# Keys and values of two cross attentions: projected for all batches at once in split fp32r and kept in DRAM, instead of batch by batch in fp32

## What is computed

```
q = (x @ Wq)                       # 256 -> 16 heads of 64
k = (context @ Wk); v = (context @ Wv)   # 192 -> 1024, 77 rows per batch
attn = softmax(q k^T / 8)
out = (attn v) @ Wo + bo
x = layernorm(x + out)
```

## Time and profile before

| what | value |
|---|---|
| median of 3 runs | 1628.12 us |
| the three runs | 1628.12, 1632.04, 1611.5 us |
| profiled execution, first to last instruction | 1625.5 us |
| busy: TensorE matmul (PE) | 1396.0 us, 86% |
| busy: weight load (PEld) | 1133.9 us, 70% |
| busy: VectorE (DVE) | 986.7 us, 61% |
| busy: ScalarE (ACT) | 637.4 us, 39% |
| busy: GpSimd (POOL) | 421.8 us, 26% |
| DMA moved | 82.25 MB, mean 51 GB/s |

### The profile page before, as it was taken

How to read it: one execution, slowest core, us unless ns; L and a number is a source line. 1 busy time by engine, 2 the same in 40 slices (tenths; PEclk the granted TensorE clock), 3 DMA queues, 4 the chain that set the end, 5 groups by cost and what they waited for, 6 DMA issues and landing times.

```text
span 1625.5 us, 28296 instructions
## 1 busy us (share of the span) xinstructions
PE 1396.0 (86%) x12184; PEld 1133.9 (70%) x12184; DVE 986.7 (61%) x1739; ACT 637.4 (39%) x743; POOL 421.8 (26%) x434
## 2 busy tenths in 40 slices
PE   5899998998969999996799699879979957878885
PEld 5688887887848889995488468748756845556553
DVE  5766756756636446776555836765583646556563
ACT  3554344434532335652344245234424511422413
POOL 2230120300311744664024412702421240000000
PEclk9999999999979999998799899979999977977868
DMA  9100000000040225872000100100000020111000
GB/s 378 61 1 1 1 1 1 1 1 1 1 181 27 77 80 193 280 228 72 1 1 32 34 1 1 61 6 1 21 20 1 1 117 2 40 29 39 2 14 14
DMA packets 28493, 82.25 MB, mean 51 GB/s; under 512 B 3152, under 2 KB 13008, under 8 KB 27344
## 3 DMA queue, kind: packets, MB, share of 16 engines
q1 hardware_dynamic: 25296, 72.05, 12.4%
q0 software_dynamic: 3072, 8.39, 1.6%
HBM read 53.95 MB, written 26.48 MB: 49 GB/s over the span
## 4 chain that ended last, share of the span: by engine, by line
PE 33%; DVE 15%; ACT 3%; POOL 2%; issue 1%; DMA 0%; POOLq 0%; DVEq 0%; ACTq 0%; another core or an unknown queue 0%
DVE sm L1520 7%; PE ps L644 5%; PE ps L1008 4%; PE ps L1014 4%; PE ps L114 3%; PE ps L116 3%; PE ps L115 3%; PE ps L989 2%; PE ps L759 2%; DVE m L1509 2%; PE ps L775 2%; PE ps L656 2%; PE ps L1128 2%; DVE m L1896 1%; ACT m L1188 1%
## 5 line engine op out<-in xcount | busy, mean ns | idle before, releaser
L1188 ACT ACTIVATE m<-ps 128x1024 f32<-128x1024 f32 (+4 forms) x248 | 183.9, 758 | 342.1 <-PE ps L116 156.3
L1520 DVE TENSOR_REDUCE sm<-ps 128x8 f32<-128x2048 f32 (+1 forms) x128 | 193.5, 1531 | 44.3 <-PE ps L989 42.6
L2124 POOL TENSOR_SCALAR sm<-sm 128x2 f32<-128x2 f32 x40 | 8.7, 218 | 764.5 <-DVE sm L1538 764.5
L1509 DVE TENSOR_TENSOR r<-ps,r 128x512 fp32r<-128x512 f32 (+1 forms) x159 | 116.2, 739 | 138.9 <-ACT r L1188 136.6
L1188 ACT ACTIVATE r<-ps 128x512 fp32r<-128x512 f32 (+1 forms) x159 | 101.3, 640 | 237.4 <-PE ps L644 117.6
L1406 ACT ACTIVATE m<-ps 128x2048 f32<-128x2048 f32 x64 | 119.6, 1877 | 150.7 <-PE ps L1008 150.7
L644 PE MATMUL ps<-cst,m 128*77 128x128 f32 (+2 forms) x1024 | 143.1, 281 | 26.6 <-ACT m L1188 5.6
L644 PEld LDWEIGHTS ps<-cst,m 128*77 128x77 f32 (+2 forms) x1024 | 116.0, 148 | 60.1 <-issue 20.2
L114 PE MATMUL ps<-r,w0h 128*128 128x256 f32 (+1 forms) x416 | 122.2, 294 | 17.9 <-DVE r L1509 13.6
L989 PE MATMUL ps<-m 32*128 32x256 f32 x1024 | 104.0, 545 | 37.2 <-DVE sm L1520 22.2
L115 PE MATMUL ps<-r,w0h 128*128 128x256 f32 (+1 forms) x416 | 118.9, 286 | 0.0
(11 more groups left out here) (241 smaller groups left out, 3603.5 us busy)
## 6 DMA issues: line engine op xcount, KB each, us to landing
raw<-wu_dram SPq DMA_DIRECT2D x20, 768.0 KB
keep_dram<-m SPq DMA_DIRECT2D x8, 768.0 KB, 3.2
m<-keep_dram SPq DMA_DIRECT2D x8, 768.0 KB, 4.9
xs_dram<-small SPq DMA_DIRECT2D x2, 2944.0 KB, 32.8
ys_dram<-m SPq DMA_DIRECT2D x23, 256.0 KB, 3.1
room<-wu_dram SPq DMA_DIRECT2D x7, 768.0 KB, 5.5
rt<-xs_dram SPq DMA_DIRECT2D x16, 256.0 KB, 3.7
w1raw<-w_dram SPq DMA_DIRECT2D x1, 3840.0 KB, 15.2
```

Of the source, the lines that this page charges most:

```text
L1188: return act.activation(o, i, ACT.Copy)
L1509: return dve.tensor_tensor(o, a, b_, op)
L1520: return dve.tensor_reduce(o, i, AX.X, op, **kw)
```

## The change

The context of all eight batches (616 columns, padded to 640) is loaded once as `ctxA` and `ctxB`, split into high and low parts, and the weights Wk and Wv are loaded raw and split, for layer 0 in the places of `wq` and `wo` (which are loaded and split after it), for layer 1 over the first 4096 columns of the same tile. `keys_values(L, u)` computes unit u of nine: units 0 to 3 are keys (four pieces of 308 columns each), units 4 to 8 are values (two pieces of 512 columns each); every piece is `mm5`, five fp32r matmuls. That is 16 pieces of keys and 10 of values per layer. Each piece is copied from PSUM to one of three slots of `stage`, and each unit is stored to DRAM (`kd`, `vd`); each batch loads its K (two DMAs) and V (one) back.

In layer 0 the nine units stand where the values and keys of batches 0 and 1 stood; batches 2 to 7 have empty steps there. In layer 1 all nine stand behind the last step of the first stage, with ACT copying and one bank in four in turn; POOL and ACT split their weights in `xattn` of batch 7. The second stage has empty steps where values and keys stood, V has a tile of its own and K lies in `w1f`, set to zero once.

The file defines the three tables twice. The first `FIRST` and `SECOND` have new numbers; behind them stands the line `CT = mybir.ActivationFunctionType` and then the constants and the tables again, with the numbers of the kernel before. Python keeps the second definition, so the program's steps run in the order of the old tables; `CT` is set to 640 further down.

```diff
+FIRST = {
+    "POOL": [0, 3, 5, 10, 11, 11, 12, 12, 12, 12, 12, 12, 13, 16, 17, 20, 21],
...
+CT = mybir.ActivationFunctionType
...
-CP = 78
-CW = 98
+CT = 640
+KW = CK * B // 2
+NSLOT = 3
+SLOT = 2 * B * CK
...
+def mm5(pe, o, a, b, ab, bb):
+    pe.matmul(o, a[0], b[0], start=True, stop=False)
+    pe.matmul(o, a[0], b[1], start=False, stop=False)
+    pe.matmul(o, a[1], b[0], start=False, stop=False)
+    for i, (l, r) in enumerate((l, r) for l in ab for r in bb):
+        m = pe.matmul(o, l, r, start=False, stop=i == 1)
+    return m
...
+            v.V = st.v1[0:CK, :] if L else m[0:CK, 0:1024]
+            v.Kf = w1f[:, 1232 * st.i:1232 * st.i + 1232] if L else m[:, 1024:2256]
+            v.K = v.Kf.rearrange("p (h c n) -> p c h n", h=2, c=8)
...
+            def store_kv(L, u):
+                slot, done, _ = slot_of(L, u)
+                sp.wait_ge(*kv_ev[L].at(L, u, 3 if u < 4 else 1))
+                if u < 4:
+                    sp.dma_start(kd[L].rearrange("b p n -> p b n")[:, :, 154 * u:154 * u + 154], slot.rearrange("p (b n) -> p b n", b=B)).then_inc(done, 16)
+                else:
+                    sp.dma_start(vd[L, P * (u - 4):P * (u - 3), :], slot[:, 0:1024]).then_inc(done, 16)
+
+            def stored(L):
+                for i in range(NSLOT):
+                    sp.wait_ge(d_slot[i], 16 * 3 * (L + 1))
+
+            def load_kv(L, b):
+                st = streams[b % 2]
+                v = x_views(st, L)
+                for h in range(2):
+                    r = slice(64 * h, 64 * h + 64)
+                    sp.dma_start(v.Kf[r, 616 * h:616 * h + 616], kd[L, b, r, :]).then_inc(d_kv[L][st.i], 16)
+                sp.dma_start(v.V, vd[L, CK * b:CK * b + CK, :]).then_inc(d_kv[L][st.i], 16)
...
+            load_kw("k0", P0["wq"][0], 0, 2048)
+            load_kw("v0", P0["wo"][0], 2048, 2048)
             load0("wout")
-            sp.dma_start(ctxT[:, 0:3 * B * CP], ctx_in).then_inc(d_ctx, 16)
-            sp.dma_start(w0f[:, 280:], w0f_in[:, 280:]).then_inc(d_kv, 16)
             sp.dma_start(xres[:, 4 * D:], x_in[:, 4 * D:]).then_inc(d_x[1], 16)
+            for u in range(4):
+                store_kv(0, u)
             load0("wq")
+            for u in range(4, 9):
+                store_kv(0, u)
             load0("wo")
+            stored(0)
+            for b in range(2):
+                sp.wait_ge(*streams[b].x_pool[0].at(b, "kz"))
+                load_kv(0, b)
...
+            for b in range(2, B):
+                sp.wait_ge(*streams[b % 2].x_pe[0].at(b - 2, "o3"))
+                load_kv(0, b)
+            for st in streams:
+                sp.wait_ge(*st.l0_pe.at(st.batches[-1], "proj"))
+            load_kw("kv1", 0, 4096, 4096)
...
             fetch(0)
             fetch(1)
+            for u in range(9):
+                store_kv(1, u)
...
+            def keys_values(L, u):
+                for s in range(4 if u < 4 else 2):
+                    q = KVQ[L, u, s]
+                    o, turns = kv_bank(L, q), 4 if L else 2
+                    if q >= turns:
+                        pe.wait_ge(*kv_ev[L].at(*KVK[q - turns, L]))
+                    if u < 4:
+                        c, r = slice(128 * (2 * u + s // 2), 128 * (2 * u + s // 2) + 128), slice(KW * (s % 2), KW * (s % 2) + KW)
+                        wa, wb = kv_weights(L, 0)
+                        m = mm5(pe, o[:, 0:KW], cols(wa, A, c), cols(ctxA, A, r), cols(wb, A, c), (ctxB[:, r],))
+                    else:
+                        t, r = slice(128 * (u - 4), 128 * (u - 3)), slice(512 * s, 512 * s + 512)
+                        wa, wb = kv_weights(L, 1)
+                        m = mm5(pe, o, cols(ctxA, A, t), cols(wa, A, r), (ctxB[:, t],), cols(wb, A, r))
+                    m.then_inc(kv_pe.up(L, u, s), 1)
...
-                values(st, b, 0, bank(st, 1), 0)
-                yield
-                pe.wait_ge(*kv_done.at(b, "v0"))
-                values(st, b, 0, bank(st, 1), 1)
-                yield
-                pe.wait_ge(*kv_done.at(b, "v1"))
-                keys(st, b, 0, bank(st, 1), 0)
-                yield
-                pe.wait_ge(*st.l0_dve.at(b, "sp"))
-                keys(st, b, 0, bank(st, 2), 1)
-                yield
+                if b == 0:
+                    for i in range(2):
+                        pe.wait_ge(*streams[i].l0_act.at(i, "z"))
+                    pe.wait_ge(*ctx_s["lo"].at("b"))
+                    pe.wait_ge(*kw_s["lo"].at("k", 0))
+                elif b == 1:
+                    pe.wait_ge(*kw_s["lo"].at("v", 0))
+                for us in ([0], [1], [2], [3]) if b == 0 else ([4, 5], [6], [7, 8], []):
+                    if b < 2:
+                        for u in us:
+                            keys_values(0, u)
+                    yield
...
             in_turn(*(x0_all(st) for st in streams), FIRST["PE"])
 
+            pe.wait_ge(*streams[0].x_dve[0].at(B - 2, "add"))
+            pe.wait_ge(*kw_s["lo"].at("kv", 1))
+            for u in range(9):
+                keys_values(1, u)
+            for q in range(22, 26):
+                pe.wait_ge(*kv_ev[1].at(*KVK[q, 1]))
...
+                if b == 1:
+                    act.wait_ge(d_ctx, 16 * 2)
+                    copy(ctxA[0][:, :], ctxA_raw[:, :]).then_inc(ctx_s["hi"].up("a"), 1)
+                    copy(ctxB[:, :], stage[:, 2 * SLOT:2 * SLOT + CT]).then_inc(ctx_s["hi"].up("b"), 1)
+                    split_kw("k", 0, d_kw["k0"], P0["wq"][0], 2048)
+                    split_kw("v", 0, d_kw["v0"], P0["wo"][0], 2048)
+                    split0("wout")
...
+                if not L and b == 0:
+                    split0("wo")
+                if not L and b == B - 1:
+                    split_kw("kv", 1, d_kw["kv1"], 0, 4096)
...
+            for u in range(9):
+                slot, free, n = slot_of(1, u)
+                act.wait_ge(free, n)
+                for s in range(4 if u < 4 else 2):
+                    act.wait_ge(*kv_pe.at(1, u, s))
+                    copy(*kv_target(1, u, s)).then_inc(kv_ev[1].up(1, u, s), 1)
...
+                def keys_values(us):
+                    for u in us:
+                        slot, free, n = slot_of(0, u)
+                        if n:
+                            dve.wait_ge(free, n)
+                        for s in range(4 if u < 4 else 2):
+                            dve.wait_ge(*kv_pe.at(0, u, s))
+                            dve.tensor_copy(*kv_target(0, u, s)).then_inc(kv_ev[0].up(0, u, s), 1)
+
+                if b < 2:
+                    keys_values([4, 5] if b else [0, 1])
+                yield
+                if b < 2:
+                    keys_values([6, 7, 8] if b else [2, 3])
...
-                if L:
-                    pool.wait_ge(*st.a_dve.at(b, "oT"))
-                    pool.memset(v.Kf, 0.0).then_inc(sig.up(b, "kz"), 1)
+                if not L and b == 0:
+                    split0("wo")
+                if not L and b == B - 1:
+                    split_kw("kv", 1, 0, 4096)
...
-            pool.memset(ctxT[:, 3 * B * CP:], 0.0).then_inc(ctx_pad.up("pad"), 1)
-            pool.wait_ge(d_cst, 16)
-            for name in ("wxp", "wout"):
-                split0(name)
             for st in streams:
                 pool.memset(x_views(st, 0).Kf, 0.0).then_inc(st.x_pool[0].up(st.i, "kz"), 1)
+            pool.wait_ge(d_cst, 16)
+            split0("wxp")
+            pool.wait_ge(*streams[0].l0_dve.at(0, "cv33"))
+            pool.wait_ge(*ctx_s["hi"].at("a"))
+            pool.tensor_tensor(ctxA[1][:, :], ctxA_raw[:, :], ctxA[0][:, :].bitcast(F32), ALU.subtract).then_inc(ctx_s["lo"].up("a"), 1)
+            pool.wait_ge(*ctx_s["hi"].at("b"))
+            pool.wait_ge(*ctx_s["lo"].at("a"))
+            pool.tensor_tensor(ctxB[64:128, :], stage[64:128, 2 * SLOT:2 * SLOT + CT], ctxB[64:128, :].bitcast(F32), ALU.subtract).then_inc(ctx_s["lo"].up("b"), 1)
+            pool.wait_ge(*ctx_s["lo"].at("b"))
+            split_kw("k", 0, P0["wq"][0], 2048)
+            pool.wait_ge(*streams[1].l0_dve.at(1, "cv33"))
+            split_kw("v", 0, P0["wo"][0], 2048)
+            split0("wout")
...
+            pool.memset(w1f[:, 0:2464], 0.0).then_inc(k1_zero.up("zero"), 1)
```

213 lines of the change are left out of this document (122 added, 91 removed).

## The result

The changed kernel takes 1674.5 us (median of five runs, 1667.9 to 1677.4) against 1628.1 before: a ratio of 1.030, 95% interval 1.025 to 1.035, so slower. The forecast was 1662 with a range of 1625 to 1685. The profiled execution spans 1666.0 us, 40.5 more than before.

The account below looks back on a forecast made before the run. The stages were taken as nearly full of matmuls, with missing time in chains through other engines; removed work was mostly filler. Terms summed to +34 on the 1625.5 us span, 1659.5, plus 2.6 for the median: 1662, range 1625 to 1685.

Parts of the forecast that it names:

- Pair 1, +21: First pair of layer 0: GpSimd splits, 26 pieces and VectorE copies delay the scores of batch 0 by 21 us.
- `wo` +3: First pair: splitting `wo` on ACT and GpSimd ahead of stream 0's bias and p0 costs 3 us.
- Pairs 2 to 4, -9: Layer 0's later pairs: without values and keys each saves 3 us, the rest of their matmul time becoming waiting.
- Split in pair 4, +16: End of first stage: GpSimd's split for layer 1 between p0 and p1 delays the turning of P by 16 us.
- Between the stages, +15: Last layernorm's add to first turned x: layer 1's matmuls, copies, weight splits and slot waits add 15 us.
- Memset +2: Second stage's first batch: two memsets of K on GpSimd stand where the batch needs it, costing 2 us.
- second stage -14: Second stage's four pairs: without values and keys each saves 3.5 us, since scores wait for stream 1's layernorm.
- that TensorE bounds the stages: Rival, 8%: in the pairs, matmul time removed from TensorE comes off the total, giving 1569 us.
- Neither port nor clock bites: Rival, 30%: pair 1 costs only +10, pairs 2 to 4 give -15, second stage -18; 1641 us.
- The clock falls wherever filler went: Rival, 14%: the pairs give nothing because TensorE's clock drops where work was removed; 1685 us.
- That the new orders were not in effect: Rival given no chance, already in the sum: old tables apply; with new ones pair 1's +21 would be smaller.

Follow-up runs that it names:

- dve_split: Changed kernel with the low parts of the context and layer 0's Wk and Wv computed on VectorE instead of GpSimd: 1670.1 us, ratio 1.025.
- stub_pair1: Changed kernel with the five matmuls of each layer 0 key and value piece cut to the first: 1662.6 us, ratio 1.021.
- copies_late: Changed kernel with VectorE's copies of units 2 and 3 moved behind the mixer steps `sp`, `dl` and `yf` of batch 0: 1667.1 us, ratio 1.024.
- late_split: Changed kernel with GpSimd's split of layer 1's Wk and Wv moved behind p3, the last scaling, of batch 7: 1656.2 us, ratio 1.017.
- slots2: Changed kernel with eight slots instead of three for layer 1's units, ScalarE waiting only for stores of units 1 to 4: 1661.4 us, ratio 1.021.
- less_kv: Kernel before, with layer 1's key and value matmuls for batches 2 to 7 cut to a stub, waits and copies kept: 1623.6 us, ratio 0.998.
- dummy_work: Changed kernel with unread matmuls, 32 per batch, put back where the second stage's values and keys stood: 1682.1 us, ratio 1.033.

## Why the prediction was right

By its own steps:

- **Pair 1, +21 and `wo` +3**: +25.4, and +21 to +22 in the other executions of the same program. The three causes named (GpSimd beside VectorE, more pieces, `sp` behind sixteen copies) are shown by dve_split, stub_pair1 and copies_late. But they don't add up: against the changed kernel's own 110.5, each alone, taken away, gives 3, 7 and 6 us of the 25.4, since another takes its place or the clock falls. That the size depends on who wins the port was not forecast. One wait was not named: ScalarE copies `B` of batch 1 behind `yr` of batch 0, which waits for `yf`, and so `Bc` of batch 1 comes 6.6 us late. That the scores come so near the forecast 106 is in part luck: in late_split (106.6) `Bc` of batch 0 came at 44.8 for 48.7, some 4 us early, and from `sp` to `turn_x` it took 27.1 us for the 23.2 allowed, some 4 us late, the unnamed wait among them. `wo` by itself wasn't tried.
- **Pairs 2 to 4, -9**: -9.6, and -6.1 to -8.3 in the other executions with the old orders. The bound of -5.1 a pair was nearly reached once (-4.7).
- **Split in pair 4, +16**: +16.2, of which 14.67 is one wait in the trace. late_split gives 10.6 of it back and shows ScalarE's part behind it.
- **Between the stages, +15**: +21.9. This is the term that was mis-sized: "1.5 for slots that wait for their store" measured 8.6 + 1.9 + 1.5. The bound of +22 held it, though its reason, half clock at the start, was another one: the granted clock was 1.00 from 480 to 492 us. I had priced the wait without asking what a store takes when it is issued right behind the experts' weights: 13.6 us in the median where layer 0's took 6.5. The other part, 22.5 + 0.6 + 0.2 + 3.0 = 26.3, measured 26.0 in slots2.
- **Memset +2, second stage -14**: -2.9 and -9.4 and -1.2, together -13.5 where -12 was forecast. The memset took 2.15 us, but at 795.2, where nobody waited for it: that term is nothing, and the -2.9 are in a stretch that took 366.4 to 371.4 us in five executions with the same steps there (373.8 before).
- **Sum**: +34 against +40.5; the stretch between the stages is 6.9 of the difference. The median then lies 8.5 us above the profiled span, not 2.6. So 1662 came out as 1674.5, and what was nearly even between "within" and "slower" fell to slower.

The rivals: that TensorE bounds the stages would have taken 102 us from the pairs (47 and 55), and was to decide from half of that on; they lost 22, and less_kv and dummy_work, which change nothing else, show the same. "Neither port nor clock bites" is refuted by the 9.58 us and by the first stage's clock of 0.91, where it was 0.98. "The clock falls wherever filler went" holds as a mechanism: 0.98 to 0.91 in the first stage, 0.95 to 0.90 in less_kv. But its price was a part of the gain, not all of it. The Trainium skill ("TensorE: Matmul & The Clock Gate", "HAM oscillation — how this bites in real kernels") says that idle gaps let the gate drop the clock; these clocks agree, and that both gains go to about nothing by it was not borne out (-9.6 and -13.5). That the new orders were not in effect mattered more than I had allowed: with them the same change costs 0.8% instead of 3.0%.

## What to carry to other kernels

Before work is taken off the busiest engine, look for what ends last at that place: in the seven pairs of batches where nothing new came, 106 us of matmuls left TensorE and gave some 22 us back, while 45 us of new ones with their splits and stores, in the first pair and between the stages, cost over 60. A one-off preparation in front of a pipeline costs every engine's share of it (here 26.0 us where 12.4 stood, with no wait for a store), and one instruction on a slow engine between two steps of a chain (8.8 us of split, +16) cost more than all four pairs of the second stage saved. When a file carries a table twice, compare the order that the program really has, not the one that the diff shows.

## What the runs showed of the hardware that was not expected

- A gap ahead of a burst shows again in the burst's clock. In dve_split TensorE was idle 5.1 us ahead of `Bc`, in slots2 0.9; though it started 1.3 us earlier, it ran at 0.79 instead of 1.00 in the following 18 us and was 0.4 us behind at `Bc` of batch 1.
- The same store lands very differently: keys (616 KB as 1024 rows of 616 bytes) in 6.5 us (median) in layer 0, and in 13.6 between the stages, behind two loads of 768 KB; values (512 KB) in 2.7 us after the keys, and in 8 us (slots2) when queued close to them.
- Who is held at the port is not fixed by the program: the same split took 4.8 us beside a VectorE that took 11.3 for 4.8 us of work, or 9.1 beside an undisturbed one, four times each in eight executions. In both sorts the profile has VectorE's row start 0.16 to 0.17 us before the split. With GpSimd as the winner, what waits on VectorE comes 2 to 5 us later; so small edits are read from their own wait, not from a later mark.
